# Graph layers on one core: whole rows unpacked into two row buffers, one bias product in bf16, another order of packing, weights and last output groups

## The chip, the core and the metric

The kernel runs on one core of one Trainium2 chip. The metric is the device time of one launch in microseconds; the lower the better. Every engine of the core has its own queue of instructions, kept in order, and the queues wait for one another through semaphores.

## What is computed

`x` is 8192 x 64, `adj` is an 8192 x 8192 matrix of zeros and ones, stored as f32 (268 MB). There are two graph layers, each followed by a residual and a layer norm:

```
deg = sum(adj, axis=1) + 1
z   = concat(x, (adj @ x + x) / deg) @ W0 + b0
h   = layernorm(x + relu(z) / ||relu(z)||)
g   = concat(h, adj @ h / (sum(adj, axis=1) + 1)) @ W1.T
out = layernorm(h + g)
```

The second layer needs `adj @ h`, and `h` of a row is known only when the first layer of that row is done.

## The kernel before, in words

**Tiles.** `adj` is read once. It is 64 block rows (128 rows each) of 4 chunks of 128 x 2048 f32, 1 MB a chunk, into a ring of six slots (`a_in`). SyncE issues the loads; a slot is free again when VectorE and ScalarE have both read it.

**One block row n, in the main stage.** For each chunk c:

- VectorE `compare(n, c)` turns the chunk into fp8 ones (`e8`, L737); ScalarE `sum_codes(n, c)` sums the bits of the same chunk as a guard against other values (L542).
- TensorE `pack_chunk(n, c)` packs eight rows into one byte by 16 small products with powers of two (`p_ps`, L346). ScalarE `take_packed(n, h)` copies each half row of them to `pk` as bytes (L551), GpSimd `keep` stores what later rows need (L1096).
- VectorE `unpack(n, h)` expands half a row of bytes into `t_sb`, the transposed matrix as fp8, by eight shift-and-mask instructions (L744), for the row before. `t_sb` holds one row. A half may be overwritten when TensorE has summed the same half of the row before.
- TensorE `sum_quarter(n, i)` multiplies 16 blocks of `t_sb` with `xh` (L360): the columns of x, split in a high and a low part, the degree, and for the blocks whose h is already known the columns of h @ W1 as well. So a product is 129 columns wide for new blocks and 257 for known ones. ScalarE `take_sums` copies the result to `agg`.

**Groups of four rows (e).** When four rows are summed, `mean`, `transpose_cat`, `dense`, `norm`, `residual`, `normalise`, `transpose_h`, `dense_h`, `low_part` and `begin_acc` compute the first layer and the start of the second. `dense` has, for each of its four rows, one f32 product with the weights (L393) and one f32 product of a row of ones with the bias (L396). Two calls of `root` on GpSimd raise small tiles to the power -0.5 in between (L1088).

**Catching up.** For rows done before h of some blocks was known, `unpack_piece`, `catch_up` (L378) and `add_piece` do the missing products from the stored bytes, a piece in each row from 12 on. Seven segments (`START`) set which rows and blocks.

**Tail.** After the last row, 16 steps of `unpack_tail`, `tail_sums` (L428) and `add_tail` do what is left for all 64 rows, in eight output groups of eight rows. The last eight steps complete a group each. For it ScalarE squares (L601), VectorE reduces (`variance`, L877, L878), GpSimd takes the root (L1103), ScalarE scales (`finish`, L611, eight instructions), and SyncE writes.

**Order.** It is written out by hand in each engine's queue; nothing plans it. TensorE in row n: pack 0, sum of row n-1 quarter 0, pack 1, quarter 1, first catch-up, pack 2, quarter 2, second catch-up, pack 3, quarter 3. VectorE in row n: compare 0, unpack of row n-1's first half, `normalise` (where it is due), add_piece, compare 1, unpack_piece, norm, compare 2, unpack of the second half, mean, compare 3, residual or the end of a group.

Of the kernel before, what the change touches and what calls it, by code (L numbers as in the profile page):

```python
# [114 lines left out]
def gnn_kernel(nc, x, adj, w0, b0, w1, out):  # L115
    ctx = ExitStack()
    with ctx:
# [12 lines left out]
        t_sb = sb("t_sb", [P, NB, P], FP8)  # L130
# [13 lines left out]
        h_sb = sb("h_sb", [P, BR, F], F32)  # L144
        h_t = sb("h_t", [F, BR, P], F32)
# [12 lines left out]
        w1_raw = sb("w1_raw", [F, P], F32)  # L158
        w1_sb = sb("w1_sb", [P, F], F32)
        w2_sb = sb("w2_sb", [F, 2 * F], F32)  # L160
        b0_sb = sb("b0_sb", [1, F], F32)

        x_in = xl[:, :, 0:F]
# [8 lines left out]
        sqf = t_sb[:, :, :].rearrange("p b i -> p (b i)").bitcast(F32).rearrange("p (s k f) -> p s k f", s=4, f=F)  # L172
# [18 lines left out]
        s_w2 = sem("s_w2")  # L191
        s_xhi = sem("s_xhi")
# [32 lines left out]
        s_o = sem("s_o")  # L225
        s_out = [sem(f"s_out{i}") for i in range(4)]
# [21 lines left out]

        def lows(n):

            return low(row_seg(n))

        agg_flat = agg[:, :, :, :].rearrange("p a k f -> p (a k f)")
        hs_flat = half_sum[:, :, :].rearrange("p n c -> p (n c)")
# [49 lines left out]
        @block.sync  # L304
        def _(sp):
            for n in range(NB):
                for c in range(NC):
                    t = n * NC + c
                    if t >= R:
                        sp.wait_ge(s_e, t - R + 1)  # L310
                        sp.wait_ge(s_half, t - R + 1)
                    sp.dma_start(a_in[:, t % R, :], adj_v[n, :, c * CH:(c + 1) * CH]).then_inc(s_in[t % R], 16)

            for g in range(NV):
                sp.wait_ge(s_o, g + 1)
                sp.dma_start(out_g[g, :, :, :], o_sb[:, g % 4, :, :]).then_inc(s_out[g % 4], 16)
            for i in range(4):
                sp.wait_ge(s_out[i], 16 * NV // 4)

            def general_sp():  # L320
                sp.sem_inc(g_out, 16)
                for q in range(NC):
                    sp.dma_start(g_feat[:, q * CB:(q + 1) * CB, 0:F], x_v[:, q * CB:(q + 1) * CB, :]).then_inc(g_x, 16)
                for layer in range(2):
                    with sp.Fori(0, NB) as n:
                        for c in range(NC):
                            sp.wait_ge(g_tps, n * GQ + (layer * NB * GQ + 1))
                            sp.dma_start(a_in[:, c, :], adj_v[bass.ds(n, 1), :, c * CH:(c + 1) * CH]
                                         .rearrange("a p c -> (a p) c")).then_inc(g_in[c], 16)
                with sp.Fori(0, NE) as e:  # L330
                    sp.wait_ge(g_o, e + 1)
                    sp.dma_start(out_v[bass.ds(e, 1), :, :, :].rearrange("a p k f -> (a p) k f"),
                                 o_sb[:, 0, 0:BR, :]).then_inc(g_out, 16)
                sp.wait_ge(g_out, 16 * NE + 16)
            if_bad(sp, general_sp)

        @block.tensor
        def _(pe):
# [11 lines left out]
            def sum_quarter(n, i):  # L350

                if i % 2 == 0:
                    pe.wait_ge(s_t, n * 2 + i // 2 + 1)
                if i == 0 and n >= 2:
                    pe.wait_ge(s_agg, n - 1)
                if n == 0:
                    pe.wait_ge(s_xlo, i + 1)
                for b in range(i * CB, (i + 1) * CB):
                    at = 0 if b < lows(n) else HP
                    last = nc.tensor.matmul(s_ps[:, n % 2, at:GW], t_sb[:, b, :], xh[:, b, at:GW],  # L360
# [4 lines left out]
                if i % 2:  # L365
                    last.then_inc(s_sum, 1)
# [33 lines left out]
            def dense(e):  # L400
# [3 lines left out]
                dense_products(cat_t, w0_sb, True).then_inc(s_zps, 1)  # L404

            def transpose_h(e):
                pe.wait_ge(s_hn, e + 1)
                for k in range(BR):
                    last = nc.tensor.transpose(c_ps[0:F, k, :], h_sb[:, k, :], ident[:, :])  # L409
# [65 lines left out]
            pe.wait_ge(s_w, 48)  # L475
            nc.tensor.transpose(c_ps[:, 0, 0:F], w1_raw[:, :], ident[0:F, 0:F])
# [5 lines left out]
            for n in range(NB):  # L482
# [3 lines left out]
                for c in range(NC):  # L486
# [3 lines left out]
                    if n == START[seg(n)] and n and c == 0:  # L490
                        pe.wait_ge(s_glo, low(seg(n)) // BR)
# [9 lines left out]
            e = NE - 1  # L501
            for c in range(NC):
# [25 lines left out]
        def _(act):  # L528
            act.dma_start(w0_sb[:, :], w0[:, :]).then_inc(s_w, 16)
            act.dma_start(w1_raw[:, :], w1[:, :]).then_inc(s_w, 16)  # L530
            act.dma_start(b0_sb[0:1, :], b0.unsqueeze(0)).then_inc(s_w, 16)
# [13 lines left out]
            def take_packed(n, h):  # L545

                act.wait_ge(s_pps, n * NC + 2 * h + 2)
                if n >= 2:
                    act.wait_ge(s_t, (n - 2) * 2 + h + 1)
# [3 lines left out]
            def take_sums(n):  # L553

                e, k = n // BR, n % BR
                act.wait_ge(s_sum, n * 2 + 2)
# [47 lines left out]
            def finish(g):  # L604
# [4 lines left out]
                for k in range(TG):  # L609
# [25 lines left out]
            act.wait_ge(s_w1t, 1)  # L635
            nc.scalar.copy(w1_sb[:, :], c_ps[:, 0, 0:F])
            nc.scalar.copy(w2_sb[:, 0:F], c_ps[0:F, 2, 0:F])
            nc.scalar.copy(w2_sb[:, F:2 * F], c_ps[0:F, 1, 0:F]).then_inc(s_w1, 1)

            for n in range(NB):  # L640
                e, k = n // BR - 1, n % BR
                sum_codes(n, 0)
                if e >= 0 and k == 2:
# [6 lines left out]
                if n:  # L650
                    take_packed(n - 1, 1)
# [24 lines left out]
            for g in range(NV + 1):  # L676
                if g < NV:
                    squares(g)
                if g:
                    finish(g - 1)  # L680
            if_bad(act, general_act)

        @block.vector
        def _(dve):
# [46 lines left out]

            def compare(n, c):
# [14 lines left out]
            def unpack(n, h):  # L747

                dve.wait_ge(s_pk, n * 2 + h + 1)
                if n:  # L750
                    dve.wait_ge(s_sum, (n - 1) * 2 + h + 1)
                half = slice(h * NB // 2, (h + 1) * NB // 2)
                dst = words(t_sb[:, half, :])
                unpack_planes(lambda g: dst[:, :, g * PKW:(g + 1) * PKW],
                              pk_w[:, n % 2, :].rearrange("p (b w) -> p b w", w=PKW)[:, half, :]).then_inc(s_t, 1)
# [44 lines left out]
            def residual(e):  # L800

                dve.wait_ge(s_root, e * 2 + 1)
                for k in range(BR):
# [14 lines left out]
            def normalise(e):  # L818

                dve.wait_ge(s_root, e * 2 + 2)  # L820
                if e:
                    dve.wait_ge(s_htps, e)
                for k in range(BR):
                    ins = nc.vector.tensor_scalar(h_sb[:, k, :], y_sb[:, k, :], small[:, 4, k:k + 1],
# [55 lines left out]

            def verdict():
# [21 lines left out]
            for n in range(NB):  # L903
                e, k = n // BR - 1, n % BR
                compare(n, 0)
                if n:
                    unpack(n - 1, 0)
                if e >= 0 and k == 3:
                    normalise(e)
                if n > START[1]:  # L910
                    add_piece(n - 1)
# [18 lines left out]
                if n == 1:  # L930
                    weights()
                if 2 <= n < 6:
# [8 lines left out]
            unpack(NB - 1, 0)  # L941
            add_piece(NB - 1)
            unpack(NB - 1, 1)
# [34 lines left out]
            for g in range(NV):  # L978
                add_tail(NV + g)
# [173 lines left out]
```

## Time and profile before

| | us |
|---|---|
| median of three runs (lowest, highest) | 792.74 (792.49, 793.36) |
| the profiled execution, its own time | 794.09 |
| its span on the core | 792.3 |
| mean granted TensorE clock | 0.946 |

The profile shows one execution. The span is cut into 40 slices of 19.8 us; busy shares are given in tenths. Busy times of one engine can overlap a little from one instruction to the next, so the distance between the starts of two instructions is what one of them costs in a full queue; a duration is somewhat longer. GB/s is what the core's DMA engines moved.

### The profile page before, as it was taken

To read this page: it belongs to the slowest core of one execution; us is meant where nothing else is said; L and a number is where in the kernel's file an instruction comes from. 1 tells how busy PE (TensorE), PEld (TensorE's weight loads), DVE (VectorE), ACT (ScalarE), POOL (GpSimd) and SP (SyncE) were. 2 spreads that over 40 slices of the span, in tenths; PEclk is the share of its full clock that TensorE was granted. 3 is DMA by queue.
4 is the path that set the end of the run, shared out by engine and by line. 5 is a ranking of instruction groups with operands and counts; after the bars stand their busy time and mean duration, and the time that the engine had idled before them with its cause. 6 is when DMAs were issued, how large, how long until landed. Compare 5 with 4: busy or idle time off the path is not lost.

```text
span 792.3 us, 28217 instructions
## 1 busy us (share of the span) xinstructions
PE 697.7 (88%) x11285; PEld 638.3 (81%) x11285; DVE 709.1 (90%) x2687; ACT 621.0 (78%) x848; POOL 201.7 (25%) x302
## 2 busy tenths in 40 slices
PE   1477868888898889999999999999999999999992
PEld 0467757777787778888889989899999989889992
DVE  4699977989999999999999999989999989878894
ACT  4798887989898989898988889787878889740037
POOL 2262513535413133334222030201102020201024
PEclk9988896989999999999999999999999999999997
DMA  9999999999999999999999999999999999800004
GB/s 304 388 419 419 419 419 401 408 420 410 421 417 416 415 416 395 421 393 421 390 417 385 404 381 393 372 344 384 345 411 361 404 350 368 314 2 2 2 15 96
DMA packets 46121, 274.56 MB, mean 347 GB/s; under 512 B 12642, under 2 KB 12706, under 8 KB 13218
## 3 DMA queue, kind: packets, MB, share of 16 engines
q1 hardware_dynamic: 45184, 270.55, 86.3%
q8 instruction: 91, 1.49, 0.8%
q0 software_dynamic: 576, 2.10, 0.7%
q14 instruction: 44, 0.36, 0.1%
q10 hardware_dynamic: 226, 0.07, 0.0%
HBM read 270.60 MB, written 2.10 MB: 344 GB/s over the span
## 4 chain that ended last, share of the span: by engine, by line
PE 48%; DVE 29%; issue 8%; DMA 6%; POOL 5%; ACT 3%; ACTq 0%; DVEq 0%; POOLq 0%; SPq 0%
PE s_ps L360 22%; DVE e L737 10%; PE u_ps L378 7%; DVE t_sb L744 6%; PE p_ps L346 6%; DMA a_in<-in_adj 3%; POOL small L1088 3%; PE z_ps L396 3%; DMA xl<-in_x 3%; PE z_ps L393 3%; PE z_ps L417 2%; DVE u_sb L744 2%; PE u_ps L428 1%; PE p_ps L428 1%; DVE a_in L744 1%
## 5 line engine op out<-in xcount | busy, mean ns | idle before, releaser
L542 ACT ACTIVATE junk<-a_in 128x2048 uint8<-128x2048 uint16 x256 | 489.2, 1918 | 4.0 <-DMA a_in<-in_adj 4.0
L360 PE MATMUL s_ps<-xh,t_sb 128*128 128x129 f16 x4096 | 386.7, 250 | 18.6 <-DVE t_sb L744 15.5
L360 PEld LDWEIGHTS s_ps<-xh,t_sb 128*128 128x128 fp8e4 x4096 | 311.3, 102 | 48.4 <-DVE t_sb L744 19.4
L737 DVE TENSOR_SCALAR e<-a_in 128x2048 fp8e4<-128x2048 f32 x256 | 310.2, 1222 | 8.2 <-DMA a_in<-in_adj 7.7
L1096 POOL COPY store<-pk 128x32 uint32<-128x32 uint32 (+1 forms) x250 | 119.8, 521 | 313.2 <-ACT pk L551 313.2
L346 PE MATMUL p_ps<-pow_bf,e 128*128 128x16 bf16 x4096 | 142.5, 170 | 51.7 <-DVE e L737 48.8
L346 PEld LDWEIGHTS p_ps<-pow_bf,e 128*128 128x128 fp8e4 x4096 | 128.6, 97 | 68.8 <-DVE e L737 62.7
L744 DVE TENSOR_SCALAR t_sb<-pk 128x128 uint32<-128x128 uint32 x1024 | 150.8, 219 | 6.5 <-ACT pk L551 6.0
L1088 POOL TENSOR_TENSOR small<-small,minus_half 128x4 f32<-128x4 f32 x32 | 65.3, 2040 | 228.0 <-DVE small L798 176.4
L378 PE MATMUL u_ps<-xh,u_sb 128*128 128x128 f16 x1488 | 99.1, 218 | 0.0
L378 PEld LDWEIGHTS u_ps<-xh,u_sb 128*128 128x128 fp8e4 x1488 | 88.9, 97 | 1.2
L551 ACT CAST pk<-p_ps 128x512 uint8<-128x512 f32 x128 | 74.5, 582 | 1.9 <-PE p_ps L346 1.9
L744 DVE TENSOR_SCALAR u_sb<-store 128x128 uint32<-128x128 uint32 (+5 forms) x416 | 60.4, 217 | 0.0
L542 ACT ACTIVATION_READ_ACCUMULATOR junk<-a_in 128x1 f32 x256 | 51.6, 202 | 0.0
L566 ACT COPY cat_t<-c_ps 128x512 f32<-128x512 f32 x16 | 9.4, 587 | 37.3 <-PE c_ps L388 37.3
L560 ACT COPY agg<-s_ps 128x257 f32<-128x257 f32 (+1 forms) x64 | 23.7, 370 | 6.5 <-PE s_ps L363 6.5
L396 PE MATMUL z_ps<-b_sb,ones_f 1*128 1x64 f32 x128 | 28.6, 304 | 0.0
L794 DVE SCALAR_TENSOR_TENSOR q_sb<-r_sb 128x64 f32<-128x64 f32 x64 | 10.6, 221 | 19.9 <-ACT r_sb L574 19.9
L393 PE MATMUL z_ps<-w_sb,cat_t 128*128 128x64 f32 x128 | 28.3, 304 | 0.0
L574 ACT ACTIVATE r_sb<-z_ps 128x256 f32<-128x256 f32 x16 | 6.1, 384 | 28.2 <-PE z_ps L396 28.2
L582 ACT COPY h_t<-c_ps 64x512 f32<-64x512 f32 x16 | 9.3, 580 | 23.3 <-PE c_ps L409 23.3
L744 DVE TENSOR_SCALAR a_in<-store 128x256 uint32<-128x256 uint32 x128 | 26.9, 285 | 0.0
(102 smaller groups left out, 512.6 us busy)
## 6 DMA issues: line engine op xcount, KB each, us to landing
a_in<-in_adj SPq DMA_DIRECT2D x256, 1024.0 KB, 8.9
xl<-in_x POOLq DMA_DIRECT2D x4, 512.0 KB, 15.8
out_h<-e SPq DMA_DIRECT2D x8, 256.0 KB, 2.6
w_sb<-in_L_gnn_W ACTq DMA_DIRECT2D x1, 32.0 KB
w_raw<-in_L_gnn_W ACTq DMA_DIRECT2D x1, 32.0 KB
b_sb<-in_L_gnn_b ACTq DMA_DIRECT2D x1, 0.2 KB
```

The costliest lines, as they stand in the source:

```text
L346: last = nc.tensor.matmul(p_ps[:, c // 2, at:at + PK], e8[:, c, b * P:(b + 1) * P], pow_bf[:, :], start=True, stop=True)
L360: last = nc.tensor.matmul(s_ps[:, n % 2, at:GW], t_sb[:, b, :], xh[:, b, at:GW], start=(b == 0), stop=False)
L378: last = nc.tensor.matmul(u_rows[:, r, :], u_sb[:, r * W + b, :], xh[:, low(q - 1) + b, 0:HP], start=(b == 0), stop=(b == W - 1))
L393: last = nc.tensor.matmul(z_flat[:, k * F:(k + 1) * F], src[:, k, :], w[:, :], start=True, stop=not bias)
L396: last = nc.tensor.matmul(z_flat[:, k * F:(k + 1) * F], ones_f[0:1, :], b0_sb[0:1, :], start=False, stop=True)
L542: nc.scalar.activation(junk[:, t % 2, :], halves[t % R], ACT.Copy, scale=1.0 / 128, accum_out=half_sum[:, n, c:c + 1]).then_inc(s_half, 1)
L551: nc.scalar.copy(pk[:, n % 2, h * 512:(h + 1) * 512], p_ps[:, h, :]).then_inc(s_pk, 1)
L560: nc.scalar.copy(agg[:, e % 2, k, at:GW], s_ps[:, n % 2, at:GW]).then_inc(s_agg, 1)
L737: nc.vector.tensor_scalar(e8[:, c, :], a_in[:, t % R, :], 1.0, None, ALU.is_equal, saturate=False).then_inc(s_e, 1)
L744: ins = nc.vector.tensor_scalar(plane(g), src, by, BIT4, op, ALU.bitwise_and)
L1088: nc.gpsimd.tensor_tensor(small[:, dst, :], small[:, src, :], minus_half[:, 0:BR], ALU.pow).then_inc(s_root, 1)
L1096: ins = nc.gpsimd.tensor_copy(stored(s, n, 1), pk_w[:, n % 2, at:at + WIDTH[s] * PKW])
```

## The change

- **Row buffers.** `t_sb` holds two whole rows. `unpack(n)` expands a whole row in eight instructions of 128x256 words, placed behind compare 1; it may start when row n-2 is summed. TensorE's quarter comes one place later: pack 0, quarter 3 of row n-2, pack 1, quarter 0 of row n-1, and so on; the catch-up stands behind packs 2 and 3. ScalarE takes the second packed half one `sum_codes` earlier. `add_piece` and `unpack_piece` move one compare later.
- **Bias.** Once, in row 2, VectorE splits b0 into three bf16 parts whose sum is b0 (16 small instructions). `dense` starts with one bf16 product of 3 x 128 ones with these parts, 256 columns wide for all four rows, and adds the four f32 products with the weights to it.
- **Start.** TensorE packs row 0 before it transposes the second layer's weights; ScalarE copies these behind row 0. Two more small loads bring b0 three times.
- **Buffers.** `h_sb`, `h_t`, `w1_raw` are gone; the same data lie in `y_sb`, `cat_t` and `agg`. `residual` rather than `normalise` waits for the transposes of the group before.
- **Last groups.** `variance(g-2)` stands ahead of `add_tail(8+g)`; both of variances 5 and 6 stand ahead of the last `add_tail`. The last group's squares and sums are eight instructions of VectorE, and the last scaling is shared: four instructions on ScalarE, four on VectorE.

```diff
-        t_sb = sb("t_sb", [P, NB, P], FP8)
+        t_sb = sb("t_sb", [P, 2, NB, P], FP8)
+        def quarter(n, c):
+            return (n - 1, c - 1) if c else (n - 2, 3)
             def sum_quarter(n, i):
-                if i % 2 == 0:
-                    pe.wait_ge(s_t, n * 2 + i // 2 + 1)
+                if i == 0:
+                    pe.wait_ge(s_t, n + 1)
+                if n + 1 == START[seg(n + 1)] and n and i * CB < lows(n):
+                    pe.wait_ge(s_glo, min(lows(n), (i + 1) * CB) // BR)
...
-                dense_products(cat_t, w0_sb, True).then_inc(s_zps, 1)
+                if e == 0:
+                    pe.wait_ge(s_b0, 1)
+                nc.tensor.matmul(z_flat[:, 0:BR * F], ones_bf[:, :], b0_rows[:, :, :].rearrange("p k f -> p (k f)"),
+                                 start=True, stop=False)
+                for k in range(BR):
+                    last = nc.tensor.matmul(z_flat[:, k * F:(k + 1) * F], cat_t[:, k, :], w0_sb[:, :],
+                                            start=False, stop=(k == BR - 1))
+                last.then_inc(s_zps, 1)
...
                     pack_chunk(n, c)
-                    if n:
-                        sum_quarter(n - 1, c)
+                    if n > 1 or c:
+                        sum_quarter(*quarter(n, c))
-                    if n >= START[1] and c in (1, 2):
-                        catch_up(n, c - 1)
+                    if n >= START[1] and c >= 2:
+                        catch_up(n, c - 2)
...
             for n in range(NB):                      # ScalarE
+                if n == 1:
+                    take_weights()
                 sum_codes(n, 0)
+                if n:
+                    take_packed(n - 1, 1)
...
-                if n:
-                    take_packed(n - 1, 1)
                 if n >= 2:
                     take_sums(n - 2)
...
-            def unpack(n, h):
+            def unpack(n):
-                dve.wait_ge(s_pk, n * 2 + h + 1)
-                if n:
-                    dve.wait_ge(s_sum, (n - 1) * 2 + h + 1)
+                dve.wait_ge(s_pk, n * 2 + 2)
+                if n >= 2:
+                    dve.wait_ge(s_sum, n - 1)
...
             for n in range(NB):                      # VectorE
                 compare(n, 0)
-                if n:
-                    unpack(n - 1, 0)
                 if e >= 0 and k == 3:
                     normalise(e)
-                if n > START[1]:
-                    add_piece(n - 1)
                 compare(n, 1)
-                if n >= START[1]:
-                    unpack_piece(n)
+                if n:
+                    unpack(n - 1)
+                if n > START[1]:
+                    add_piece(n - 1)
                 if e >= 0 and k == 2:
                     norm(e)
                 compare(n, 2)
+                if n >= START[1]:
+                    unpack_piece(n)
-                if n:
-                    unpack(n - 1, 1)
...
             for g in range(NV):
+                if g >= 2:
+                    variance(g - 2)
+                if g == NV - 1:
+                    variance(g - 1)
                 add_tail(NV + g)
                 if g + 12 < 2 * NV:
                     unpack_tail(g + 12)
-                if g:
-                    variance(g - 1)
-            variance(NV - 1)
+            last_variance()
+            last_finish()
```

## Rows read from the trace of the kernel before

**Rows 1.** The page: busy tenths, granted clock and GB/s in 40 slices.

```profile
PE   1477868888898889999999999999999999999992
DVE  4699977989999999999999999989999989878894
PEclk9988896989999999999999999999999999999997
GB/s 304 388 419 419 419 419 401 408 420 410 421 417 416 415 416 395 421 393 421 390 417 385 404 381 393 372 344 384 345 411 361 404 350 368 314 2 2 2 15 96
```

**Rows 2.** Stages: length, busy us (xinstructions) of PE, PEld, DVE, ACT, POOL; clock, DMA share, GB/s.

```profile
60.00:120.00 60.00, 46.49 (x798) 41.85 (x795) 54.10 (x173) 52.89 (x70) 19.15 (x44) 0.85 1.01 419
240.00:360.00 120.00, 108.37 (x1847) 98.52 (x1845) 116.12 (x465) 107.39 (x139) 38.16 (x59) 0.99 1.01 409
480.00:600.00 120.00, 119.53 (x1868) 109.36 (x1867) 111.52 (x433) 98.42 (x130) 16.12 (x24) 0.99 0.97 375
```

**Rows 3.** Waits between 400 and 700 us: who waited for whom, us, times, longest.

```profile
PEld p_ps L346 <- DVE e L737: 2.2, 6, 0.6
PE p_ps L346 <- DVE e L737: 0.5, 2, 0.3
DVE t_sb L744 <- ACT pk L551: 2.5, 7, 0.4
```

**Rows 4.** Timeline of TensorE: first weight product of five groups: start, us.

```profile
203.41 0.39 PE L393 MATMUL z_ps<-w_sb,cat_t 128*128 128x64 f32 x2
...
244.03 0.39 PE L393 MATMUL z_ps<-w_sb,cat_t 128*128 128x64 f32 x2
...
368.17 0.39 PE L393 MATMUL z_ps<-w_sb,cat_t 128*128 128x64 f32 x2
...
410.01 0.39 PE L393 MATMUL z_ps<-w_sb,cat_t 128*128 128x64 f32 x2
...
680.02 0.39 PE L393 MATMUL z_ps<-w_sb,cat_t 128*128 128x64 f32 x2
```

**Rows 5.** Groups by line and shape.

```profile
L744 DVE TENSOR_SCALAR t_sb<-pk 128x128 uint32<-128x128 uint32 x1024 | 150.8, 219 | 6.5 <-ACT pk L551 6.0 <-PE s_ps L363 0.4
L396 PE MATMUL z_ps<-b_sb,ones_f 1*128 1x64 f32 x128 | 28.6, 304 | 0.0
...
L808 DVE TENSOR_SCALAR small<-small 128x4 f32<-128x4 f32 x16 | 2.8, 174 | 0.5
```

**Rows 6.** Timeline of VectorE: unpackings and what starts behind them, and `normalise`.

```profile
332.38 1.26 DVE L744 TENSOR_SCALAR t_sb<-pk 128x128 uint32<-128x128 uint32 x8 [0.35 <-ACT pk L551]
...
336.86 1.23 DVE L737 TENSOR_SCALAR e<-a_in 128x2048 fp8e4<-128x2048 f32 x1
338.00 1.17 DVE L744 TENSOR_SCALAR t_sb<-pk 128x128 uint32<-128x128 uint32 x8
339.25 0.98 DVE L824 TENSOR_SCALAR h_sb<-y_sb,small 128x64 f32<-128x64 f32 x4
...
758.79 1.70 DVE L744 TENSOR_SCALAR a_in<-store 128x256 uint32<-128x256 uint32 x8
760.40 0.68 DVE L870 TENSOR_TENSOR xl<-u_ps,xl 128x512 f32<-128x512 f32 x1
```

**Rows 7.** Timeline of TensorE: a group's `dense` and what follows, at 634 us.

```profile
634.27 0.39 PE L393 MATMUL z_ps<-w_sb,cat_t 128*128 128x64 f32 x2
634.59 0.43 PE L396 MATMUL z_ps<-b_sb,ones_f 1*128 1x64 f32 x2
634.95 0.43 PE L393 MATMUL z_ps<-w_sb,cat_t 128*128 128x64 f32 x2
...
637.12 0.56 PE L346 MATMUL p_ps<-pow_bf,e 128*128 128x16 bf16 x16
637.54 2.84 PE L360 MATMUL s_ps<-xh,t_sb 128*128 128x257 f16 x16
640.17 0.62 PE L346 MATMUL p_ps<-pow_bf,e 128*128 128x16 bf16 x16
640.64 2.49 PE L360 MATMUL s_ps<-xh,t_sb 128*128 128x257 f16 x16
642.98 1.05 PE L378 MATMUL u_ps<-xh,u_sb 128*128 128x128 f16 x16
```

**Rows 8.** The same behind the `dense` of 545 us.

```profile
547.74 0.56 PE L346 MATMUL p_ps<-pow_bf,e 128*128 128x16 bf16 x16
548.16 1.95 PE L360 MATMUL s_ps<-xh,t_sb 128*128 128x257 f16 x16
549.95 0.55 PE L346 MATMUL p_ps<-pow_bf,e 128*128 128x16 bf16 x16
```

**Rows 9.** Stretches right behind three of the `dense` blocks (columns as in rows 2).

```profile
548.00:551.20 3.20, 3.20 (x53) 2.87 (x50) 2.55 (x15) 3.20 (x6) 1.98 (x2) 1.00 0.84 323
...
638.00:641.20 3.20, 3.20 (x33) 2.46 (x31) 2.82 (x17) 3.20 (x5) 2.13 (x2) 0.56 0.92 320
...
723.30:726.50 3.20, 3.20 (x35) 3.20 (x36) 2.68 (x15) 0.38 (x1) 1.01 (x1) 0.57 0.00 0
```

**Rows 10.** The end: timeline of the last groups.

```profile
779.26 0.69 DVE L870 TENSOR_TENSOR xl<-u_ps,xl 128x512 f32<-128x512 f32 x1
...
780.59 0.61 ACT L601 ACTIVATE t_sb<-xl 128x512 f32<-128x512 f32 x1
...
783.66 0.69 DVE L877 TENSOR_REDUCE fvar<-t_sb 128x8 f32<-128x512 f32 x1 [1.54 <-ACT t_sb L601]
784.63 1.64 POOL L1103 TENSOR_TENSOR fvar<-fvar,minus_half 128x8 f32<-128x8 f32 x1 [0.79 <-DVE fvar L878]
786.30 2.02 ACT L611 ACTIVATE e<-xl,fvar 128x64 f32<-128x64 f32 x8 [0.41 <-POOL fvar L1103]
```

**Rows 11.** Timeline of VectorE: two squares with sums of `norm`.

```profile
548.26 0.23 DVE L794 SCALAR_TENSOR_TENSOR q_sb<-r_sb 128x64 f32<-128x64 f32 x1 [1.13 <-ACT r_sb L574]
...
548.41 0.22 DVE L794 SCALAR_TENSOR_TENSOR q_sb<-r_sb 128x64 f32<-128x64 f32 x1
```

More of the change, by code:

```diff
@@ L157, in gnn_kernel @@
         w0_sb = sb("w0_sb", [P, F], F32)
-        w1_raw = sb("w1_raw", [F, P], F32)
         w1_sb = sb("w1_sb", [P, F], F32)
         w2_sb = sb("w2_sb", [F, 2 * F], F32)
-        b0_sb = sb("b0_sb", [1, F], F32)
+        b0_sb = sb("b0_sb", [3, F], F32)
+        b0_rows = sb("b0_rows", [3, BR, F], BF16)
+        ones_bf = sb("ones_bf", [3, P], BF16)
+        h_t = cat_t[0:F, :, :]
+        b0_rest, b0_sum, b0_one = (q_sb[0:3, i, :] for i in range(3))
+        b0_part = q_sb[0:3, 3, 0:F // 2].bitcast(BF16)
         x_in = xl[:, :, 0:F]
@@ L474, in _ @@
             pe.wait_ge(s_pow, 1)
-            pe.wait_ge(s_w, 48)
-            nc.tensor.transpose(c_ps[:, 0, 0:F], w1_raw[:, :], ident[0:F, 0:F])
+            for c in range(NC):
+                pack_chunk(0, c)
+            pe.wait_ge(s_w, 80)
+            nc.tensor.transpose(c_ps[:, 0, 0:F], w1_raw, ident[0:F, 0:F])
             for i in range(2):
@@ L480, in _ @@
             pe.wait_ge(s_w1, 1)
-            for n in range(NB):
+            for n in range(1, NB):
                 e, k = n // BR - 1, n % BR
@@ L529, in _ @@
             act.dma_start(w0_sb[:, :], w0[:, :]).then_inc(s_w, 16)
-            act.dma_start(w1_raw[:, :], w1[:, :]).then_inc(s_w, 16)
-            act.dma_start(b0_sb[0:1, :], b0.unsqueeze(0)).then_inc(s_w, 16)
+            act.dma_start(w1_raw, w1[:, :]).then_inc(s_w, 16)
+            for i in range(3):
+                act.dma_start(b0_sb[i:i + 1, :], b0.unsqueeze(0)).then_inc(s_w, 16)
             halves = [a_in[:, i, :].bitcast(U16).rearrange("p (b two) -> p b two", two=2)[:, :, 1]
@@ L608, in finish @@
                     act.wait_ge(s_out[g % 4], 16)
-                for k in range(TG):
+                for k in range(TG if g < NV - 1 else TG // 2):
                     n = g * TG + k
@@ L675, in _ @@
             take_g(e)
-            for g in range(NV + 1):
-                if g < NV:
+            for g in range(NV):
+                if g < NV - 1:
                     squares(g)
@@ L730, in weights, with bias @@
                                         ALU.mult).then_inc(s_w2, 1)
+            def bias():
+                link(nc.vector.memset(ones_bf[:, :], 1.0))
+                link(nc.vector.tensor_copy(b0_rest, b0_sb[:, :]))
+                link(nc.vector.memset(b0_sum, 0.0))
+                for i in range(3):
+                    link(nc.vector.tensor_copy(b0_part, b0_rest))
+                    link(nc.vector.tensor_copy(b0_one, b0_part))
+                    link(nc.vector.scalar_tensor_tensor(out=b0_sum, in0=b0_one, scalar=ident[0:3, i:i + 1],
+                                                        in1=b0_sum, op0=ALU.mult, op1=ALU.add))
+                    link(nc.vector.tensor_tensor(b0_rest, b0_rest, b0_one, ALU.subtract))
+                nc.vector.tensor_copy(b0_rows[:, :, :], b0_sum.unsqueeze(1).to_broadcast([3, BR, F])
+                                      ).then_inc(s_b0, 1)
             def compare(n, c):
@@ L931, in _ @@
                     weights()
+                if n == 2:
+                    bias()
                 if 2 <= n < 6:
```

63 lines of the change are left out of this document (41 added, 22 removed).

## The prediction, made before the change was run

> **What bounds the kernel now.** I read the slices first. The reader is to see a relay: up to slice 15 the DMA moves 400 to 420 GB/s while VectorE is at nine tenths and TensorE at eight; then TensorE is at nine tenths to the end while the GB/s fall to 350 and 400 by turns [rows 1]. The windows put numbers to it: 419 GB/s at 60 to 120 us, 409 with VectorE busy 116.1 of 120 us, then 375 with TensorE busy 119.5 of 120 [rows 2]. Third come the waits of the late stretch: in 300 us TensorE waits 0.5 us for VectorE's compare, and its weight loads 2.2 [rows 3]. So TensorE paces the kernel from about 400 us on, and what its queue loses is lost from the end.
>
> The period of a group of four rows shows the same without busy shares. Between the starts of `dense`: 40.6 us (203.41 to 244.03), 41.4 on average over the next three (to 368.17), 41.8 (to 410.01), and 45.0 on average over six (to 680.02) [rows 4]. Sixteen chunks, 16.78 MB, at 419 GB/s take 40.0 us; that is the floor of a group.
>
> **Bias, on TensorE.** A group has four pairs of a weight and a bias product. In rows 7 the first pair starts at 634.27 and the first pack behind the four pairs at 637.12: 2.85 us. A bias product takes 0.36 of it (634.59 to 634.95), so the four cost 1.43 us of queue. In their place stands one bf16 product of 256 columns. No row shows it; the nearest is a product of 257 columns, 16 of them from 548.16 to 549.95, 0.11 us each [rows 8]. The bounds are 0.03 us (16 packs of 16 columns from 547.74 to 548.16) and 0.36 (an f32 bias product). I take 0.15, between, near the row of the same width, with something for the change of weights: 1.28 us saved in each group. Seven groups have their `dense` in the stretch that TensorE paces (410 to 680; first and last in rows 4): 9.0 us. Bounds 7.5 and 9.8.
>
> **The clock behind `dense`.** After the block of 634 us the next 16 sums run from 637.54 to 640.17 and 16 more from 640.64 to 642.98, 2.63 and 2.34 us [rows 7]; behind the block of 545 us the same 16 take 1.79 [rows 8]. The windows tell why: TensorE is busy all the time in both, but the granted clock is 0.56 in one, a stretch mostly at 1.2 GHz, and 1.00, which is 2.4 GHz, in the other [rows 9]. Before it fell the engine had done nothing but `dense`. So it goes behind five of the seven blocks in the stretch (410, 454, 498, 634, 680; rows 9 show one of them) and behind that of the tail at 720; not behind those of 545 and 590. Each costs 2.63 + 2.34 - 2 x 1.79 = 1.4 us, with the slower pack 1.45. The changed block is 4 x 0.36 + 0.15 = 1.6 us rather than 2.85. Since the long one brings the clock down five times in seven, one of little over half its length should seldom do so. I take all five as gone: 7.3 us. Bounds: 0 (the same five stay) and 7.3.
>
> The Trainium skill (TensorE: Matmul & The Clock Gate, section "HAM oscillation — how this bites in real kernels") ties a fall of the clock to gaps in which the engine is idle. The trace differs: in the stretches at 0.56 and ahead of them TensorE was busy throughout. By that rule the shorter `dense` would give no clock back, and the gain would be 8.9 us smaller; that is rival 1.
>
> **Unpacking, on VectorE.** Half a row takes 1.14 to 1.25 us of queue (338.00 to 339.25, of which the last 0.1 is a wait; 332.38 plus 1.18 to the next) and 1024 instructions 219 ns each by the group [rows 5, 6]. I use 1.1 for a half. Eight instructions of 128x256 exist in the tail: 758.79 to 760.40, 1.61 us [rows 6]. A row saves 2 x 1.1 - 1.6 = 0.6, a group 2.4. One thing is given back: `normalise` stood behind compare 0 and a half unpacking and started 0.1 late, at 339.25. Now it stands behind compare 0 alone, which ends its turn at 338.00, so VectorE idles 1.2 us for GpSimd's root. The wait of 0.35 us for the packed half [rows 6] goes, since ScalarE takes it one `sum_codes` earlier. Net 1.5 us a group.
>
> Where does that count? Only where VectorE paces: the groups from 244 to 410, 41.4 and 41.8 us long. They would go to 40.0 to 40.3, the DMA floor. (3 x 1.4 + 1.8) less 4 x 0.2 is 5.2, with 0.4 for the group before 5.6; I take 4.5. Bounds 2 and 6. Late, where TensorE paces, it is cover: VectorE needs 111.5 of 120 us now [rows 2], in a group of 45.0 that is 41.8, less 2.4 plus 1.2 is 40.6, against 42.5 that TensorE will need (45.0 - 1.28 - 1.2). That is close, and its waits for ScalarE at `norm` and `low_part` come on top. I charge 1.5 us over the stretch (bounds 0 and 9).
>
> **The moved waits.** TensorE's quarter 0 waits for the whole row's unpacking. That stands behind `take_packed(n-1, 1)`, which needs the last pack of row n-1. From that pack to quarter 0 TensorE has two quarters, a catch-up and two packs, at least 0.9 + 0.9 + 0.9 + 0.8 = 3.5 us; the copy (0.5) and unpacking (1.6) take 2.1. Hidden where TensorE is late; where the DMA paces, TensorE has slack of 10 in 120 us [rows 2]. `take_sums(n-2)` on ScalarE now waits for a quarter issued behind pack 0 of row n. Behind it stand two `sum_codes`, on which slots of the ring depend. ScalarE needs 98.4 of 120 us, 37 of 45 in a group, some 2 us a row spare. Cost 0 (rival 3 if not). `residual`'s and `mean`'s new waits are for work long done. The `s_glo` waits stand a pack later than before: 0.
>
> **Start.** Sixteen small VectorE instructions in row 2, 0.17 us each by a small instruction's row [rows 5], with the gaps 3.5 us, beside the guard of x. The ring lets VectorE lag by some of it, and it is made up by 0.6 a row. Before it, ScalarE no longer stops for the weights in front of its first chunk, but the loads there run at what x leaves. I take +1 (bounds -1 and +3).
>
> **Tail.** `dense` of the last group stands in TensorE's path: 1.28 less. The 64 products behind it run at a clock of 0.57 [rows 9], with 5.2 us rather than 3.6: 1.6 less. Together 2.9. **Last groups:** up to variance 4 the new order is the old one, differently written. Then the last `add_tail` (779.26 before [rows 10]) waits behind variance 6, which needs squares that end at 781.2 [rows 10]: it moves to 782.0. Add 1.35, eight squares at 0.15 [rows 11], one small one, GpSimd 1.64, half a scaling 1.0: the end of scaling at 787.8 against 788.3 now [rows 10]. 0.5 less (bounds -1 and 1.5).
>
> **Sum**, against 794.1, the profiled execution's own time: 9.0 + 7.3 + 4.5 - 1.5 - 1 + 2.9 + 0.5 = 21.7, so 772.4. The median of the runs lies 1.4 below that execution: **771.0**.
>
> **Rivals.**
>
> 1. *The clock stays low behind `dense`.* For it: where in time the block falls, not only its length, decides (545 and 590 did not bring it down). Against: the block nearly halves. 7.3 + 1.6 less of gain: 780.
> 2. *VectorE becomes the bound late.* For it: 40.6 busy of 42.5 and a longer order (whole unpacking between compare 1 and 2). Against: it waits for TensorE there, not the other way [rows 3]. If groups end at 43.8, six and a half of them lose 8.5: 779.
> 3. *Slower: ScalarE blocks at `take_sums`.* Its place is row n, between `sum_codes` 1 and 2; it waits for quarter 3 of row n-2, and TensorE waits for the packed half that ScalarE takes three instructions later. Once the wait is longer than ScalarE's 2 us, each row of the 52 from row 12 on pays the excess. At 0.42 us a row it eats the gain of 21.7; at 0.8 the time is 771 + 42 = 813, or about 800 if only the late half pays more. Against: quarter 3 of row n-2 ends 1.8 us into TensorE's row.
> 4. *The change does not speed TensorE up,* because the new bias product between f32 ones costs as much as four (0.36 x 4): 9.0 + 1.3 + 8.9 us less gain, 790.
>
> **Chances.** Forecast 0.58, rival 1 0.18, rival 2 0.14, rival 3 0.06, rival 4 0.04. The forecast's own range, by the bounds above, is 765 to 776; rivals 1 and 2 reach to 783, and leaving out 3, 4 and the very edges makes 764 to 783. A measurement of this kernel can tell 0.2%, 1.6 us, from no change: faster 0.92, same 0.02, slower 0.06.
>
> **What would show it.** `dense` 1.6 us from first to last product, periods of 40.0 to 40.3 us before 400 and about 42.5 after; clock 1.00 in the windows behind the late `dense` blocks; GB/s near 395 at 480 to 600; 1.6 us for an unpacked row; `normalise` waiting about 1.2 us for GpSimd. Wrong if TensorE shows waits for `t_sb` in the late stretch, or if the clock at 0.56 comes back at other places as often as before.

## The result: slower, 811.2 against 792.6 us

| | median us (runs) | range |
|---|---|---|
| before | 792.62 (4) | 790.67 to 793.36 |
| changed | 811.22 (4) | 809.90 to 813.38 |

The ratio is 1.0237, with a 95% interval of 1.0213 to 1.0261: 19 us slower. The forecast was 771.0 with a range of 764 to 783, and slower had a chance of 0.06. It was wrong in sign.

The slices of the changed kernel, to be read against [rows 1]:

```profile
PE   0367777878787879898898989999999999999992
DVE  4699878788898988888888899898978788867894
PEclk9989787878999999999899999999998989989996
GB/s 304 390 420 420 420 421 419 419 420 396 420 404 422 391 419 343 422 345 422 348 390 344 401 394 380 372 366 382 353 382 359 354 365 339 273 2 2 2 15 93
```

In slices 3 to 9 it moves 419 to 421 GB/s, the rate of the kernel before at its best. From slice 16 on the rate drops to some 345 in every other slice, while *both* VectorE and TensorE are less busy than they were. No engine is busy all the time; they wait for one another. The windows say so in numbers (columns as in [rows 2]):

```profile
60.00:120.00 60.00, 45.05 (x815) 41.28 (x813) 52.25 (x122) 55.29 (x74) 18.26 (x44) 0.86 1.01 420
...
240.00:360.00 120.00, 101.40 (x1718) 90.18 (x1716) 104.12 (x359) 101.81 (x132) 25.49 (x56) 0.96 0.97 392
...
480.00:600.00 120.00, 114.90 (x1877) 105.59 (x1878) 107.71 (x335) 98.87 (x127) 15.62 (x22) 1.00 0.98 373
```

From 240 to 360 us VectorE fell from 116.1 to 104.1 us busy and TensorE from 108.4 to 101.4, and yet less data came in, 392 GB/s instead of 409. Part of the fall is work saved: as an estimate, 0.6 us of unpacking in each of some eleven rows and 1.7 us of `dense` in each of three groups, about 7 us of VectorE and 5 of TensorE. The rest is waiting. Who waited for whom over the whole span (us, times, longest):

```profile
DVE t_sb L784 <- ACT pk L572: 56.4, 39, 3.7
...
PE s_ps L373 <- DVE t_sb L784: 40.6, 40, 3.0
...
ACT agg L581 <- PE s_ps L376: 32.6, 28, 6.0
```

Three waits, and they close a ring: VectorE waits for the packed half that ScalarE copies (6.0 us before [rows 5]), TensorE for VectorE's row (15.5 before), ScalarE for TensorE's sums (6.5 before). The timeline of one row shows the first. The changed kernel behind the last pack of a row (its line first):

```profile
552.49 0.55 PE L357 MATMUL p_ps<-pow_bf,e 128*128 128x16 bf16 x16
...
553.57 0.59 ACT L587 COPY cat_t<-c_ps 128x512 f32<-128x512 f32 x1 [1.94 <-PE c_ps L400]
554.05 1.91 ACT L563 ACTIVATE junk<-a_in 128x2048 uint8<-128x2048 uint16 x1
...
555.96 0.57 ACT L572 CAST pk<-p_ps 128x512 uint8<-128x512 f32 x1
556.15 0.28 PE L418 MATMUL z_ps<-b_rows,ones_bf 3*128 3x256 bf16 x1
556.36 1.10 PE L421 MATMUL z_ps<-w_sb,cat_t 128*128 128x64 f32 x8
556.56 1.71 DVE L784 TENSOR_SCALAR t_sb<-pk 128x256 uint32<-128x256 uint32 x8 [2.48 <-ACT pk L572]
557.30 0.55 PE L357 MATMUL p_ps<-pow_bf,e 128*128 128x16 bf16 x16
...
559.07 1.16 PE L373 MATMUL s_ps<-xh,t_sb 128*128 128x257 f16 x9
```

The pack is done at 553.0. ScalarE copies it at 555.96, because `take_cat` and a `sum_codes` of 1.9 us stand ahead in its queue. VectorE idles 2.48 us, and the row is unpacked at 558.3, 5.2 us behind the pack. TensorE does not wait in this row: it has `dense` to do, and comes to the row's first quarter at 559.07. The second wait falls in other rows. Of its 40.6 us, 31.2 lie between 60 and 400 us; between 400 and 690 us there are six waits, 6.4 us in all, each in the fourth row of a group, where `normalise` stands ahead of the unpacking. TensorE in such a row:

```profile
662.89 0.56 PE L357 MATMUL p_ps<-pow_bf,e 128*128 128x16 bf16 x16 [0.51 <-DVE e L777]
664.51 1.76 PE L373 MATMUL s_ps<-xh,t_sb 128*128 128x257 f16 x11 [1.06 <-DVE t_sb L784]
```

### The profile page after: what moved, and what is told of

Same layout as the page of the kernel before. It is cut to its first block, busy times and chain, and to the rows that moved or that the text cites. A ratio compares the mean times of both kernels' runs of the same rounds, so it can differ in the third digit from the quotient of the medians.

```text
span 811.6 us, 27450 instructions
## 1 busy us (share of the span) xinstructions
PE 680.5 (84%) x11173; PEld 618.9 (76%) x11173; DVE 677.9 (84%) x2210; ACT 621.0 (77%) x843; POOL 163.9 (20%) x302
## 4 chain that ended last, share of the span: by engine, by line
PE 39%; DVE 28%; ACT 12%; POOL 8%; issue 8%; DMA 3%; ACTq 0%; DVEq 0%; POOLq 0%
PE s_ps L373 22%; ACT junk L563 10%; DVE t_sb L784 8%; POOL small L1151 7%; DVE e L777 6%; PE u_ps L390 6%; PE p_ps L357 5%; PE z_ps L436 3%; DMA xl<-in_x 3%; ACT pk L572 2%; DVE q_sb L851 1%; DVE y_sb L845 1%; DVE a_in L784 1%; DVE y_sb L863 1%; PE p_ps L447 1%
## 5 line engine op out<-in xcount | busy, mean ns | idle before, releaser
L373 PE MATMUL s_ps<-xh,t_sb 128*128 128x129 f16 x4096 | 389.8, 252 | 40.6 <-DVE t_sb L784 40.6
L777 DVE TENSOR_SCALAR e<-a_in 128x2048 fp8e4<-128x2048 f32 x256 | 305.8, 1221 | 7.5 <-DMA a_in<-in_adj 7.3
L784 DVE TENSOR_SCALAR t_sb<-pk 128x256 uint32<-128x256 uint32 x512 | 111.4, 289 | 56.4 <-ACT pk L572 56.4
L1159 POOL COPY store<-pk 128x32 uint32<-128x32 uint32 (+1 forms) x250 | 85.5, 383 | 343.5 <-ACT pk L572 343.5
L1151 POOL TENSOR_TENSOR small<-small,minus_half 128x4 f32<-128x4 f32 x32 | 76.1, 2378 | 254.1 <-DVE small L837 221.5
L581 ACT COPY agg<-s_ps 128x257 f32<-128x257 f32 (+1 forms) x64 | 22.8, 356 | 32.8 <-PE s_ps L376 32.6
L609 ACT CAST xh<-z_ps 128x256 f16<-128x256 f32 x16 | 6.0, 372 | 49.6 <-PE z_ps L436 49.6
L863 DVE TENSOR_SCALAR y_sb<-y_sb,small 128x64 f32<-128x64 f32 x64 | 16.1, 313 | 13.5 <-POOL small L1151 13.5
L436 PE MATMUL z_ps<-w_sb,cat_t 64*128 64x128 f32 x128 | 25.3, 355 | 0.0
L436 PEld LDWEIGHTS z_ps<-w_sb,cat_t 64*128 64x128 f32 x128 | 21.5, 251 | 4.2 <-issue 3.9
L447 PE MATMUL u_ps<-xh,a_in 128*128 128x128 f16 x384 | 22.4, 218 | 0.5 <-ACT agg L581 0.5
```

Of the source, the lines that this page charges most:

```text
L373: last = nc.tensor.matmul(s_ps[:, n % 2, at:GW], t_sb[:, n % 2, b, :], xh[:, b, at:GW], start=(b == 0), stop=False)
L436: last = nc.tensor.matmul(z_ps[:, k, :], h_t[:, k, :], w2_sb[:, :], start=True, stop=True)
L447: last = nc.tensor.matmul(v_ps[j % 3][:, r, :], v_sb[:, j % VR, r * W + b, :], xh[:, at + b, 0:HP], start=(b == 0), stop=(b == W - 1))
L777: nc.vector.tensor_scalar(e8[:, c, :], a_in[:, t % R, :], 1.0, None, ALU.is_equal, saturate=False).then_inc(s_e, 1)
L784: ins = nc.vector.tensor_scalar(plane(g), src, by, BIT4, op, ALU.bitwise_and)
L863: ins = nc.vector.tensor_scalar(y_sb[:, k, :], y_sb[:, k, :], small[:, 4, k:k + 1], small[:, 6, k:k + 1], ALU.subtract, ALU.mult)
```

## The experiments

All twelve were timed beside the kernel before on the same chip, four at a time; its median was 792.7, 791.0 and 792.0 in the three sets, so medians of different sets compare to some 1.7 us, ratios better.

| run | median us | ratio to before (95%) |
|---|---|---|
| bias alone | 779.30 | 0.9832 (0.9816, 0.9849) |
| changed, f32 bias put back | 802.75 | 1.0119 (1.0096, 1.0142) |
| all but the row buffers | 779.72 | 0.9844 (0.9826, 0.9863) |
| halves | 783.46 | 0.9889 (0.9872, 0.9906) |
| copy first | 779.21 | 0.9852 (0.9832, 0.9872) |
| both halves late | 792.34 | 1.0017 (1.0006, 1.0029) |
| whole row early, copy first | 787.53 | 0.9938 (0.9912, 0.9964) |
| `normalise` late | 805.74 | 1.0165 (1.0125, 1.0205) |
| copy first, f32 bias | 794.36 | 1.0023 (1.0002, 1.0044) |
| halves, copy first | 776.99 | 0.9814 (0.9798, 0.9830) |
| copy later | 868.38 | 1.0974 (1.0955, 1.0992) |
| copy first, row 3 early | 775.36 | 0.9793 (0.9777, 0.9810) |

### Which part costs

**Bias alone**: the kernel before with this edit, the split of b0 in row 2 and its two more loads.

```diff
-                dense_products(cat_t, w0_sb, True).then_inc(s_zps, 1)
+                nc.tensor.matmul(z_flat[:, 0:BR * F], ones_bf[:, :], b0_rows..., start=True, stop=False)
+                for k in range(BR):
+                    last = nc.tensor.matmul(z_flat[:, k * F:(k + 1) * F], cat_t[:, k, :], w0_sb[:, :],
+                                            start=False, stop=(k == BR - 1))
+                last.then_inc(s_zps, 1)
```

> The kernel before with the bias change alone. Theory A (the bias product saves TensorE 1.28 us in each group that TensorE paces, and the loss of the whole change comes from the row buffers): 792.6 less 9.0 in the seven late groups less 1.3 in the tail, and less up to 8.9 where the clock no longer falls behind the group's dense block: 774 to 783, dense 1.25 us long rather than 2.85. Rival (the bf16 product between f32 ones costs what it saves): 790 to 793.

779.3: 13.4 us faster. A late `dense`, timeline of TensorE:

```profile
669.53 0.28 PE L411 MATMUL z_ps<-b_rows,ones_bf 3*128 3x256 bf16 x1
669.74 1.10 PE L414 MATMUL z_ps<-w_sb,cat_t 128*128 128x64 f32 x8
670.68 0.55 PE L351 MATMUL p_ps<-pow_bf,e 128*128 128x16 bf16 x16
671.09 1.95 PE L365 MATMUL s_ps<-xh,t_sb 128*128 128x257 f16 x16
```

The block takes 1.15 us (669.53 to 670.68) instead of 2.85 [rows 7]. The windows, the last one right behind that block:

```profile
480.00:600.00 120.00, 118.51 (x1941) 109.55 (x1940) 116.44 (x454) 102.50 (x134) 20.07 (x24) 1.00 0.99 390
600.00:660.00 60.00, 59.56 (x961) 54.86 (x959) 57.27 (x214) 51.89 (x67) 6.12 (x7) 1.00 0.99 387
671.50:674.70 3.20, 3.20 (x43) 2.84 (x42) 2.81 (x17) 3.20 (x5) 2.14 (x2) 1.00 0.95 335
```

The clock is 1.00 throughout, where it had been 0.56 or 0.57 behind five blocks of this stretch [rows 9]. TensorE still paces, at 43.3 us a group.

**Changed, f32 bias put back:**

```diff
-                nc.tensor.matmul(z_flat[:, 0:BR * F], ones_bf[:, :], b0_rows..., start=True, stop=False)
-                for k in range(BR): ...
+                dense_products(cat_t, w0_sb, True).then_inc(s_zps, 1)
...
-                if n == 2:
-                    bias()
```

> The changed kernel with the four f32 bias products put back. Theory A: VectorE and ScalarE pace the changed kernel, so most of the bias's gain is hidden there; without it 811 becomes 812 to 820. Rival (the bias change itself slows the kernel, through its waits or its loads): below 800.

802.75, between the two: neither expectation held. The bias change, worth 13 us in the old order, *costs* 8.5 us in the new one.

**All but the row buffers**: the bias-alone kernel and

```diff
+            for c in range(NC):
+                pack_chunk(0, c)
             pe.wait_ge(s_w, 80)
...
+                if g >= 2:
+                    variance(g - 2)
+                if g == NV - 1:
+                    variance(g - 1)
                 add_tail(NV + g)
...
+            last_variance()
+            last_finish()
```

> The kernel before with bias, start and last groups changed, one row buffer and the old order. Theory A: within 2 us of the bias change alone (774 to 783), start worth -1 to +3, last groups -1.5 to +1. Rival (packing ahead of the weights or the last groups' order costs the 19 us): above 795 while the bias change alone is below 785.

779.7, within half a microsecond of the bias alone. Start and last groups together are worth nothing that can be measured. The loss is in the row buffers and the order that came with them.

### What in the row buffers costs

**Halves**: the changed kernel with

```diff
                 compare(n, 0)
+                if n:
+                    unpack(n - 1, 0)
                 if e >= 0 and k == 3:
                     normalise(e)
                 compare(n, 1)
-                    unpack(n - 1)
+                    unpack(n - 1, 1)
...
             def sum_quarter(n, i):
-                if i == 0:
-                    pe.wait_ge(s_t, n + 1)
+                if i % 2 == 0:
+                    pe.wait_ge(s_t, n * 2 + i // 2 + 1)
```

A half needs only its own packed half, and TensorE's quarters 0 and 1 need only the first half.

> The changed kernel, but VectorE unpacks the row of before in two halves, the first behind compare 0, the second behind compare 1; two row buffers and TensorE's and ScalarE's new order stay. Theory A1 (what costs is that nothing can be unpacked before ScalarE has taken the last packed half, so VectorE idles 56 us and TensorE then waits for it): most of the loss goes, 775 to 790, VectorE's wait for pk under 15 us. Rival A2 (TensorE's later quarters and ScalarE blocking at take_sums cost it): stays at 805 or more.

783.5, 27.8 us faster than changed; VectorE's wait for pk is down to 15.1 us. TensorE's and ScalarE's new order and the two buffers are still in it. Against all but the row buffers (779.7) they and the halves together make 4 us. ScalarE's wait for TensorE's sums is still 31.2 us here (32.6 in the changed kernel): the third link of the ring is not what costs the time.

**Both halves late**: the halves kernel with

```diff
                 compare(n, 0)
-                    unpack(n - 1, 0)
...
                 compare(n, 1)
+                    unpack(n - 1, 0)
                     unpack(n - 1, 1)
```

> The halves kernel (783.5) with both halves unpacked behind compare 1, in the place where the changed kernel unpacks a whole row; VectorE pays 0.5 us a row more than for a whole row. If the place costs the time: 808 to 825. Rival (the size of the unpacking, or that TensorE can start on the first half before the second is done, decides): below 795, since here too the first half is given free alone.

792.3. The rival held: VectorE does more than in the changed kernel, in the same place, and is 19 us faster. The first half needs only an earlier copy, and it can be summed while the second is made; which of the two helps more, no run tells apart. The place behind compare 1 costs the other 9 us.

**Copy first**: two lines of ScalarE's order, nothing else.

```diff
-                sum_codes(n, 0)
                 if n:
                     take_packed(n - 1, 1)
+                sum_codes(n, 0)
```

> The changed kernel, ScalarE takes the last packed half ahead of sum_codes 0 rather than behind it. Theory A1 (VectorE idles 53 us because that copy stands behind a sum_codes of 1.9 us): the wait at least halves and the time falls to 788 to 803. Rival B (the chain root, normalise, compare 1, unpack is what is late): 807 or more, with the wait for pk turned into another one.

779.2: the swap alone takes 32 us off the changed kernel (30.5 by the ratios), more than either expectation had, and undoes all of its loss. The same row of the same group in this run:

```profile
531.47 0.55 PE L357 MATMUL p_ps<-pow_bf,e 128*128 128x16 bf16 x16
...
532.54 0.59 ACT L587 COPY cat_t<-c_ps 128x512 f32<-128x512 f32 x1 [1.30 <-PE c_ps L400]
533.03 0.59 ACT L572 CAST pk<-p_ps 128x512 uint8<-128x512 f32 x1
533.50 1.93 ACT L563 ACTIVATE junk<-a_in 128x2048 uint8<-128x2048 uint16 x1
...
533.65 1.71 DVE L784 TENSOR_SCALAR t_sb<-pk 128x256 uint32<-128x256 uint32 x8 [0.92 <-ACT pk L572]
```

From the end of the pack (532.02) to the start of unpacking it is now 1.6 us instead of 3.5, and the row is ready 3.3 us behind the pack instead of 5.2. The waits, whole span:

```profile
ACT pk L572 <- PE p_ps L357: 22.1, 25, 1.7
...
DVE t_sb L784 <- ACT pk L572: 10.8, 11, 1.9
```

ScalarE now idles 22 us for TensorE's pack. It can afford to.

Where do the 32 us lie? TensorE's waits for `t_sb` between 400 and 690 us are as long as they were, 6.8 us; those for VectorE's compare fall from 5.8 to 1.0, for a VectorE that idles for pk comes later to its next compares. More of it is TensorE's clock. From the 4th and from the 13th to the 16th `dense`, each time the changed kernel first, then this one (columns as in [rows 2]):

```profile
203.80:740.58 536.78, 491.19 (x7870) 441.93 (x7869) 459.35 (x1554) 431.50 (x557) 91.68 (x161) 0.96 0.91 354
201.27:706.05 504.78, 470.73 (x7870) 432.60 (x7869) 459.97 (x1555) 430.55 (x556) 100.39 (x161) 0.99 0.94 378
...
601.42:740.58 139.16, 133.90 (x1921) 118.90 (x1920) 111.43 (x393) 94.14 (x123) 18.26 (x17) 0.93 0.71 265
579.09:706.05 126.96, 123.62 (x1921) 113.87 (x1920) 109.99 (x387) 93.67 (x124) 18.35 (x17) 1.00 0.76 293
```

Of the 32.0 us between the first two TensorE's idle time makes 11.5; for the other 20.5 it was busy longer with the same work. Before 400 us, where TensorE has slack, longer busy time need not cost anything; between the last two it does: of 12.2 us 1.9 are idle time, and the same 1921 instructions took 10.3 us more, at a mean clock of 0.93 instead of 1.00. How the clock came down is taken up below.

**Copy later**: the opposite, behind sum_codes 1, where the kernel before has it.

```diff
                 sum_codes(n, 0)
-                if n:
-                    take_packed(n - 1, 1)
...
                 sum_codes(n, 1)
+                if n:
+                    take_packed(n - 1, 1)
```

> The changed kernel with the copy one sum_codes later, behind sum_codes 1, where the kernel before has it. Theory A1 (each place of 1.9 us that the copy stands later is added to the wait of VectorE in most rows): slower than 811 by 25 us or more, over 836. Rival (the copy-first gain has another cause than the delay, as ScalarE's order against take_z): within 8 us of 811.

868.4, 57 us more:

```profile
DVE t_sb L784 <- ACT pk L572: 122.7, 46, 5.6
...
PE s_ps L373 <- DVE t_sb L784: 91.0, 50, 3.7
ACT agg L581 <- PE s_ps L376: 82.4, 39, 6.0
```

All three waits of the ring grow together. Three places of the copy give 779, 811 and 868 us: that is a dose and its answer, and it is shown that the copy's place in ScalarE's queue is the cause.

### The rest of the chain

**Whole row early**: the copy-first kernel with

```diff
                 compare(n, 0)
+                    unpack(n - 1)
                     normalise(e)
                 compare(n, 1)
-                    unpack(n - 1)
```

> The changed kernel with ScalarE's copy ahead of sum_codes 0 and the whole row unpacked right behind compare 0, ahead of normalise. Theory A1: VectorE reaches the unpacking one compare earlier and waits longer for pk, TensorE gets its row earlier; between the copy-first kernel and 5 us less than it. Rival B (normalise's wait for the root, now covered by the unpacking, is what is late): 12 us or more below the copy-first kernel.

787.5, 8 us slower than copy first, against both expectations: a whole row cannot be had so early, and VectorE waits for pk 44.0 us between 60 and 690 us. TensorE never waits for its row there, but 50.9 us for VectorE's compare, against 31.5 with the copy first alone: one wait gone is no gain where the next one grows.

**`normalise` late**: the changed kernel with

```diff
-                    normalise(e)
                 compare(n, 1)
                     unpack(n - 1)
+                    normalise(e)
...
-                    if e >= 0 and (k, c) == (3, 0):
+                    if e >= 0 and (k, c) == (3, 1):
                         transpose_h(e)
```

and `dense_h`, `take_h` and `take_g` one place later.

> The changed kernel with normalise behind compare 1 and the unpacking; transposes, dense_h and ScalarE's copies for them stand one place later. Theory A1: VectorE no longer idles for the root (12.6 us before), time 803 to 811. Rival B: below 800 and no fall of the clock behind rows of that kind.

805.7, within theory A1's range: the place of `normalise`, and with it the wait for GpSimd's root, is worth some 5.5 us (its four runs lie between 800.8 and 807.1). VectorE's wait for pk fell from 56.4 to 32.0 us with it, so the sum of a wait is no measure of its price.

**Copy first, row 3 early**: the early place in every fourth row alone, in place of the one behind compare 1.

```diff
                 if e >= 0 and k == 3:
+                    unpack(n - 1)
                     normalise(e)
```

> The copy-first kernel, but in each fourth row (k = 3), where normalise waits for GpSimd's root, the whole row is unpacked ahead of normalise. If the root's wait of 0.9 us and TensorE's wait behind it are on the path of a group: 779.2 less 16 x 0.5 to 1, 764 to 773. If they are cover for other waits: 777 to 781.

775.4, between the two ranges (764 to 773, 777 to 781): neither expectation held. The gain of 3.8 us on the copy-first kernel is half of the least that the first one had. This is the fastest kernel of the study, 17 us ahead of the kernel before. Its waits of TensorE for `t_sb` are 13.2 us, against 31.1 with the copy first alone. Its middle groups come near the floor:

```profile
240.00:360.00 120.00, 106.41 (x1871) 96.53 (x1872) 111.67 (x385) 111.04 (x143) 32.12 (x60) 0.97 1.01 417
480.00:600.00 120.00, 118.99 (x1932) 109.73 (x1929) 111.64 (x367) 103.38 (x134) 19.88 (x23) 1.00 1.00 396
```

**Halves, copy first**, the halves kernel with the two lines swapped on ScalarE:

```diff
-                sum_codes(n, 0)
                 if n:
                     take_packed(n - 1, 1)
+                sum_codes(n, 0)
```

> The halves kernel (783.5) with the copy ahead of sum_codes 0. Theory A1: it had 15 us of waits for pk, of which half goes, 777 to 782; VectorE, busy 92 percent, then paces the middle groups at 41.5 us. Rival (with the copy first, a whole row is no better than halves and the two stack): below 775.

777.0, at the edge of the first range; VectorE's wait for pk is 0.2 us.

### Why the bias change cost time in the new order

**Copy first, f32 bias**, both edits above in one kernel:

```diff
-                nc.tensor.matmul(z_flat[:, 0:BR * F], ones_bf[:, :], b0_rows..., start=True, stop=False)
+                dense_products(cat_t, w0_sb, True).then_inc(s_zps, 1)
...
-                sum_codes(n, 0)
                     take_packed(n - 1, 1)
+                sum_codes(n, 0)
```

> The copy-first kernel (779.2) with the four f32 bias products put back. With the order left as changed, putting them back made the kernel 8.5 us faster. Theory: that was because TensorE did not pace there and its idle time let the clock fall; where TensorE paces again, they cost what they did in the kernel before, 13 us: 788 to 794. Rival (in the two-buffer order the bias products cost nothing whatever ScalarE does): 776 to 782.

794.4, 0.4 us above the theory's range. With the copy first the bias change is worth 15.2 us (13.5 by the ratios, as much as in the old order), with the copy behind `sum_codes` it costs 8.5. In the changed kernel TensorE waits in the ring, and time saved in its queue becomes idle time. That idle time seems not to be free. Windows of the changed kernel in one late group, columns as before:

```profile
659.00:662.00 3.00, 3.00 (x58) 2.88 (x55) 2.10 (x6) 2.79 (x6) 1.87 (x2) 1.00 0.99 363
662.00:664.50 2.50, 0.94 (x20) 0.58 (x18) 2.50 (x10) 2.37 (x3) 0.00 (x0) 1.00 0.98 370
664.50:671.00 6.50, 6.49 (x47) 4.96 (x48) 5.37 (x17) 2.48 (x5) 0.00 (x0) 0.57 0.95 328
```

TensorE was busy 0.94 of 2.5 us, waiting for a compare and a row; then the clock is 0.57 for 6.5 us, mostly 1.2 GHz, with the engine busy throughout. The group took 47.9 us from `dense` to `dense`; groups of the same kernel without such a stretch took 45.3, and the late groups of the run with the f32 bias, which has no such stretch after 605 us, 45.7, 45.3 and 40.9, against 47.9, 47.9 and 43.4 here. That is 7.2 of the 10.5 us between the spans of the two profiled executions (8.5 between the medians); another 5.3 had come about before the first of these groups, and the tail gives 2.0 back.

That the missing bias products brought the clock down is argued from these rows; no run held the clock and changed only the idle time. And such a wait does not always do it. Two groups earlier the same two waits, 0.51 and 1.06 us, stand in the same place, and no fall followed:

```profile
569.60:572.10 2.50, 0.93 (x20) 0.73 (x20) 2.50 (x10) 2.38 (x3) 0.00 (x0) 1.00 0.92 357
```

What else decides is open.

## Why the prediction was wrong, step by step

- **The bound of the kernel before** was read rightly: taking work off TensorE's queue alone gave 13.4 us.
- **Bias, 9.0 us, and clock, 7.3 us.** Mechanism right, the size too large. All five low stretches and the tail's are gone in the bias-alone run, so rival 1 is out. The Trainium skill (TensorE: Matmul & The Clock Gate, section "HAM oscillation — how this bites in real kernels") ties a fall of the clock to gaps in which the engine is idle. The late falls of the kernel before do not agree, as TensorE was busy without a gap ahead of them; those of the changed kernel came behind gaps, though short ones (0.51 and 1.06 us). The block shrank by 1.7 us rather than 1.28: with nothing between them the four f32 weight products take 0.94 us (669.74 to 670.68), 0.23 each, where the sum had 0.36 each. The end is smaller than the forecast's 19.2 for bias, clock and tail: 13.4. Groups from the ninth on took 260.5 us for six instead of 270.0, 9.5 less. TensorE's busy time in them fell by 14.5 us, from 268.7 to 254.2; the other 4.9 became idle time, mostly waits for VectorE's compare (4.4 us, 0.5 before). VectorE, busy 116.4 of 120 us there, was close behind TensorE.
- **Unpacking on VectorE, 4.5 us.** The instructions cost what was forecast, eight of 289 ns, 1.6 us a row, and `normalise` waits 0.9 us for the root in 15 groups, rather than 1.2. The gain did not come even with the copy first: that kernel (0.9852 of the kernel before) is no faster than the one without the row buffers (0.9844). The sentence that ScalarE's wait of 0.35 us "goes, since ScalarE takes it one `sum_codes` earlier" was wrong in sign: it became 56.4 us in all.
- **The moved waits: the step that failed.** The text set "the copy (0.5) and unpacking (1.6) take 2.1" against 3.5 us of cover. It left out what stands ahead of the copy in ScalarE's queue, though the diff shows it: `sum_codes(n, 0)`, 1.9 us, and in one row of four `take_cat`, 0.5. In the row shown the chain is 5.2 us instead of 2.1. The cover was about right: 3.4 us in the shortest row in which TensorE did not wait, 6.0 in the row shown, where `dense` stands in it. So late in the kernel TensorE does not wait for that chain itself. What the text also left out is that VectorE idles inside the chain, 56.4 us in all, and comes late to its compares, to `normalise` and to the next row, for which TensorE then waits. The fall of the clock behind some of these waits, 10.3 us in the last three groups, it named only as a sign of being wrong. The term was put at 0; the swap shows that it cost 32 us. In the kernel before the copy stood one place later still and was harmless, because only the second half row needed it, and VectorE had the first half, a piece and a compare to do meanwhile. Making the row one unit tied its *first* block to its *last* copy.
- **Rival 3** had the right ring (ScalarE, TensorE's quarter, the packed half) and priced it at 800 to 813, but put its weak point at `take_sums` with a spare of 2 us a row. That wait grew to 32.6 us, and is 31.2 in the halves kernel, which is 27.8 us faster. ScalarE's spare time is an average; what counted was its order. It had 0.06.
- **Rival 2**, VectorE as the bound, did not come: it is busy 107.7 of 120 us late, less than before.
- **Start, +1, and last groups, -0.5.** Unmeasurable together, as forecast. In the trace, from the start of variance 5's reduction to the end of scaling it is 9.3 us (797.06 to 806.35) against 9.9 (778.45 to 788.32): 0.6. The size agrees in part by luck: the terms that the text names for the end add up to 787.4, not to its 787.8.
- **What would show it wrong** was named rightly: TensorE's waits for `t_sb`, and the clock coming back at other places.

## What to carry to other kernels

When two small units are fused into one, its first consumer inherits the last producer. Work the latency of that chain out through every queue it crosses, with what stands ahead of each link, not with the links' own durations. An engine with spare time on average is no cover: here a swap of two adjacent instructions on an engine that is busy 77% moved the time by 32 us, nine tenths of the 35.9 us between the best kernel of the study and the changed one.

A part that gains on its own should be measured on its own. Here a 13 us gain stood beside a loss of 32 and was itself turned into a loss by it.

## What the runs showed that was not expected

- TensorE's clock fell behind two different kinds of stretch: in the changed kernel behind one with 0.94 of 2.5 us busy, in the kernel before behind the f32 products of `dense`, with the engine busy throughout and the clock at 1.00 (and then at 0.56 [rows 9]):

```profile
634.20:637.10 2.90, 2.90 (x21) 2.38 (x17) 1.67 (x9) 1.79 (x2) 0.00 (x0) 1.00 0.97 404
```

- Four f32 products with weights take 0.94 us in a row, but 0.36 us each, 1.42 in all, when a one-row f32 product stands behind each.
- Shorter work on TensorE made the kernel slower by 8.5 us where TensorE waited in a ring with two other engines, and 13 us faster where it did not.
